# Normalising the first batch's attention on GpSimd, with the spread of the sums issued one row of maxima earlier

## The reference: one transformer layer with ternary weights

```
q, k, v = x@wqT+bq, x@wkT+bk, x@wvT+bv      # 16 heads of 8
attn    = softmax(q·k / 4) · v                # per head, over 1024 keys
x       = layernorm(x + attn@woT + bo)
h       = silu(x@w1T*s1) * (x@w2T*s2)         # 512 wide
h       = gelu(h@h1T*s); h = gelu(h@h2T*s)
out     = layernorm(x + h@w3T*s3)
```

## Time and profile before

| | us |
|---|---|
| median of 3 runs | 441.21 |
| lowest, highest | 440.68, 442.07 |
| the profiled execution | 441.35 |
| its span in the trace | 439.6 |
| granted TensorE clock, mean | 0.998 of full |

### The profile page before, as it was taken

The page is one execution under the profiler, slowest core; times in us unless marked ns, Lnnn a source line. Parts: engine busy times, 40 slices in busy tenths (PEclk is TensorE's granted clock), DMA queues, the critical chain, the costliest instruction groups (busy, mean ns, idle before and its releaser), DMA issues.

```text
span 439.6 us, 9789 instructions
## 1 busy us (share of the span) xinstructions
PE 426.9 (97%) x3498; PEld 228.3 (52%) x3498; DVE 383.8 (87%) x704; ACT 363.6 (83%) x683; POOL 106.9 (24%) x198
## 2 busy tenths in 40 slices
PE   8999999999999999999999999999999899999995
PEld 3544545444444444444445454544333588877884
DVE  6799999999999999999999999999874576657636
ACT  4497989999998999998899998998799885678762
POOL 9730110101011010101101013958111363046103
PEclk9999999999999999999999999999999999999999
DMA  5667741111131111113011111121021000000101
GB/s 161 174 204 119 281 147 28 49 28 28 48 123 25 40 37 28 28 48 123 25 40 39 26 28 49 16 41 52 10 41 49 15 8 1 1 1 3 48 1 48
DMA packets 17117, 24.89 MB, mean 57 GB/s; under 512 B 5168, under 2 KB 9008, under 8 KB 16688
## 3 DMA queue, kind: packets, MB, share of 16 engines
q1 hardware_dynamic: 16464, 23.68, 19.8%
q10 hardware_dynamic: 608, 0.59, 0.5%
HBM read 15.08 MB, written 7.60 MB: 52 GB/s over the span
## 4 chain that ended last, share of the span: by engine, by line
PE 74%; DVE 12%; ACT 4%; SPq 3%; issue 2%; DMA 2%; POOL 1%; POOLq 0%; DVEq 0%; ACTq 0%
PE ps L1366 23%; PE ps L1288 18%; PE ps L1476 16%; DVE negmax L983 11%; PE ps L1350 9%; ACT arena L663 2%; DMA parts_q<-arena 2%; PE ps L1220 2%; PE ps L1231 1%; PE ps L1420 1%; PE ps L1316 1%; PE ps L1260 1%; SPq L462 1%; SPq L434 1%; ACT v_pad L716 1%
## 5 line engine op out<-in xcount | busy, mean ns | idle before, releaser
L983 DVE TENSOR_REDUCE negmax<-ps 128x1 f32<-128x512 f32 x458 | 274.5, 683 | 1.4 <-PE ps L1288 1.3
L663 ACT ACTIVATE arena<-ps 128x512 f32<-128x512 f32 x360 | 190.3, 605 | 21.3 <-PE ps L1350 14.7
L1350 PE MATMUL ps<-qx,kx 64*128 64x512 f32 x512 | 170.0, 450 | 0.9 <-DMA qx<-mT 0.6
L1288 PE MATMUL ps<-kx,qx 61*128 61x512 f32 x468 | 159.3, 440 | 0.8 <-DMA qx<-parts_q 0.5
L1288 PEld LDWEIGHTS ps<-kx,qx 61*128 61x128 f32 x468 | 75.1, 184 | 86.7 <-DVE negmax L983 76.6
L1366 PE MATMUL ps<-arena,v_pad 128*32 128x256 f32 (+3 forms) x1328 | 104.7, 407 | 2.4 <-ACT arena L663 2.4
L663 ACT ACTIVATE hf<-ps 128x512 f32<-128x512 f32 x152 | 83.3, 602 | 9.5 <-PE ps L1350 8.0
L1350 PEld LDWEIGHTS ps<-qx,kx 64*128 64x128 f32 x512 | 78.6, 184 | 18.2 <-ACT arena L663 11.5
L1476 PE MATMUL ps<-hid,w_high 128*128 128x512 f32 (+1 forms) x296 | 68.3, 387 | 0.8 <-issue 0.4
L1476 PEld LDWEIGHTS ps<-hid,w_high 128*128 128x128 f32 x296 | 54.2, 188 | 12.4 <-issue 0.8
L1366 PE MATMUL ps<-hf,v_pad 128*32 128x128 f32 (+1 forms) x600 | 47.5, 388 | 0.0
(11 more groups left out here) (109 smaller groups left out, 333.7 us busy)
## 6 DMA issues: line engine op xcount, KB each, us to landing
qx<-parts_q SPq DMA_DIRECT2D x60, 64.0 KB, 2.1
late_sb<-in_late SPq DMA_DIRECT2D x3, 1280.0 KB, 5.7
kx<-parts_k SPq DMA_DIRECT2D x56, 64.0 KB, 2.1
parts_q<-prt SPq DMA_DIRECT2D x3, 512.0 KB, 6.4
parts_q<-arena SPq DMA_DIRECT2D x3, 512.0 KB, 8.2
xT_sb<-in_xT SPq DMA_DIRECT2D x4, 256.0 KB, 4.0
xT_sb<-arena SPq DMA_DIRECT2D x28, 32.0 KB
prt<-den SPq DMA_DIRECT2D x7, 128.0 KB
```

The costliest lines, as they stand in the source:

```text
L663: nc.scalar.activation(probs(n // HG)[:, heads(n), :], ps[:, PLAN["score", n][0], :], ACT.Exp, scale=SCALE).then_inc(exp_done, 1)
L983: nc.vector.tensor_reduce(negmax[:, t // TURNS % 2, m % 2, h * QT + q:h * QT + q + 1], ps[:, MAX_BANK + m % 4, :], AX.X, ALU.max, negate=T ...
L1288: nc.tensor.matmul(ps[:, half_bank(m), :], qx[at, slot, qc, h, q * P:(q + 1) * P], kx[at, slot, h, part * C:(part + 1) * C], start=True, s ...
L1350: nc.tensor.matmul(ps[:, bank, :], kx[at, slot, h % PAIR, kt * P:(kt + 1) * P], qx[at, slot, qc, h % PAIR, :], start=True, stop=True)\
```

## The change

GpSimd gets a function `norm(c)` with the two waits (sums spread back, attention moved) and the multiplication, and runs it for chunk 0 ahead of step 12 and for chunk 1 ahead of step 13 of its own list. VectorE loses `norm(0)` and `norm(1)` and keeps those of the second batch. SyncE issues `spread(0)` ahead of `load_max(ITERS - 1, 2)`.

```diff
+NORM_STEPS = (12, 13)
...
             load_max(ITERS - 1, 1)
             gather(0)
             move(0)
+            spread(0)
             load_max(ITERS - 1, 2)
-            spread(0)
             load_max(ITERS - 1, 3)
...
+            def norm(c):
+
+                if c == 0:
+                    pool.wait_ge(den_back[0], 16 * NG)
+                    pool.wait_ge(moved[0], MOVED[0])
+                at = slice(c * C, (c + 1) * C)
+                nc.gpsimd.tensor_tensor(attn_c[:, at], attn_c[:, at], den[:, at], ALU.mult)\
+                  .then_inc(chunk_normed, 1)
+
             for k in range(STEPS):
+                if k in NORM_STEPS:
+                    norm(NORM_STEPS.index(k))
                 if k % KT == 3 and k // KT + 1 < PER:
                     split_max(ITERS - 1, k // KT + 1)
...
             def norm(c):

-                if c == 0:
-                    dve.wait_ge(den_back[0], 16 * NG)
-                    dve.wait_ge(moved[0], MOVED[0])
                 if c == QC:
...
             dve.wait_ge(max_split, U_ALL)
-            norm(0)
-            norm(1)
             dve.wait_ge(pv_done, HF_STEPS)
```

## The result

| | before | changed |
|---|---|---|
| median, us | 441.51 (6 runs) | 444.72 (6 runs) |
| lowest, highest | 440.68, 442.07 | 444.26, 446.34 |
| ratio, 95% interval | | 1.0080 (1.0059 to 1.0100) |
| profiled execution, us | 441.35 | 444.55 |
| its span, us | 439.6 | 442.8 |

A forecast was written before the change was run, and what follows sets the result against it. The prediction took the chain through VectorE's maxima, the split and a normalisation before out_proj as the bound; +2.56 for the split less 0.57 for the normalisation gave +1.99, so 441.21 + 2.0 = 443.2 us, range 441.8 to 444.4.

The forecast's parts named there:

- The spread's start: On SyncE, the write of the sums to DRAM starts at about 293.74 us, not 299.26.
- From write to first read: On SyncE, 2.18 us from the write of the sums to the first read-back, at 295.92.
- The read-back: Four DMAs of the sums: 7.59 us from first issue to last packet plus 0.41 wake-up, so GpSimd starts at 303.92.
- GpSimd's chain: On GpSimd behind the wait: two multiplications at 1.23 us, five slices at 1.92 and a 0.05 tail, before the split.
- The split: GpSimd's split of unit 15's maxima starts at 316.03 us instead of 313.47, 2.56 late.
- Out_proj: On TensorE, out_proj starts 0.16 us behind the turn, at 318.29 against 316.30: 1.99 late.
- I carry the whole +2.0 to the end: Behind out_proj, the delay of 2.0 us reaches the end whole, with nothing made up by ScalarE or TensorE.
- VectorE's two multiplications: Taking 2 x 0.69 us from VectorE has value zero, as its flags now start when the split is done.
- Idle time that suffices: Rival: sums back on GpSimd by 301.36, split at 313.47 as before, 0.57 us won, time 440.6; chance 0.07.
- The stall partly made up: Rival: TensorE's 0.76 us of later idle time shrinks the 2.0 to 1.25, time 442.5; chance 0.13.
- The maxima's packets among the sums': Rival: unit 14's loads run among the sums' reads, sums and split 1.2 us later, +3.2, 444.4; chance 0.08.
- Unit 14's maxima as the bound: Rival: they land behind the sums, so late that TensorE stops at the group of 305.70; 444 or above; chance 0.03.

The follow-up runs named there:

- spread_only: The kernel before with only the spread of the sums issued ahead of unit 14's maxima load, both normalisations left on VectorE: 441.71 us against 441.65, ratio 1.0007.
- changed_again: The changed kernel run once more, unaltered, for a second profile: 444.05 us in one run.
- norms_late: The changed kernel with GpSimd's two normalisations ahead of its steps 18 and 19 instead of 12 and 13: 441.22 us against 441.65, ratio 0.9997.
- late_and_held: norms_late with SyncE waiting, before the load of unit 14's maxima, until the sums are back: 440.62 us in one run.
- loads_held: The changed kernel with SyncE waiting, before the load of unit 14's maxima, until the sums are back: 445.0 us in 4 runs, ratio 1.0089.
- pool_only: The changed kernel with the spread back behind the load of unit 14's maxima, normalisations still on GpSimd: 450.56 us against 441.21, ratio 1.0207.

## Why the prediction was wrong, step by step

The direction and the mechanism were right: the idle time of 7.48 us did not suffice, and the split moved from VectorE's chain to GpSimd's. Of the 3.97 us by which the end is late, 2.0 were forecast, 0.5 are missing at out_proj (the read-back), and 1.45 come behind it (the clock). Step by step, behind zero (forecast values less 278.82):

- **The spread's start.** Forecast 14.92, measured 14.91. Right, as was the move's price of nothing (spread_only).
- **From write to first read.** Forecast 2.18, measured 2.04. Between the two prices in the earlier trace rows.
- **The read-back.** "7.59 us from first issue to last packet" and 0.41: forecast 8.00, measured 8.82. Here the sum was mis-sized by 0.8. I had this as a rival with a chance of 0.08 and a price of 1.2, and dismissed it since the loads "are issued last". The profiles average 8.0 without loads behind and 8.8 with them. The Trainium skill (DMA: Bandwidth & Descriptors, Queues, rings and completion order) says that each engine takes its descriptors in ring order. I read this as if a later load could not slow the reads, which the page does not say; the measurement decides, and reads with a load issued behind them took longer. That its packets ran among theirs is not shown.
- **GpSimd's chain.** Forecast 12.11 from the first multiplication to the split, measured 12.03 (303.82 to 315.85). Each multiplication took 1.28 and its spacing was 1.23, as taken from the earlier trace rows.
- **The split.** Forecast 2.56 late, measured 3.15.
- **Out_proj.** Forecast 0.16 behind the turn, measured 0.10; 1.99 late against 2.52.
- **"I carry the whole +2.0 to the end."** This is the step that failed. It was right only that nothing is made up. I had read the clock in the earlier trace rows as 1.00 and taken it for granted, while my own sum put a 2.5 us hole into TensorE's stream. The hole cost 1.45 more (2.52 at out_proj, 3.97 at the end), and nothing more when it was filled (2.80 and 2.77). No rival priced it. Where the clock did not fall (changed_again), 2.39 at out_proj became 2.34 at the end, so the carry of the hole's own length was right.
- **VectorE's two multiplications.** Value zero, right: its flags started at 317.92, right behind the split.
- **The rivals.** Idle time that suffices: norms_late brings it about, by moving the wait and not by faster transfers, and there 0.3 of the gain reaches the end, not 0.57. The stall partly made up: no. The maxima's packets among the sums': its time, 444.4, is nearest to the measured one, but by luck, since the reads cost 0.8 and not 1.2, and the rest is the clock. Unit 14's maxima as the bound: not in the changed kernel, but it shows in late_and_held, where their load starts 5.5 us later still.

## What to carry to other kernels

A wait given to an idle engine delays everything queued behind it there. Compare the arrival of what it waits for with the due time of the last instruction behind it less all the work between, not with the engine's idle share; and put the wait behind as much of the other work as there is.

When a change makes TensorE wait for some microseconds, price the hole twice: by its length, and by the matmuls behind it at half clock, 1.45 to 1.83 us here where the clock fell. Before spending a gain on the chain, look at which engine is next: here half of it was given back at the scores that wait for ScalarE.

## What the runs showed of the hardware that I had not expected

- TensorE's granted clock (1.2 instead of 2.4 GHz) fell to half behind a hole of 3.1 us, of 3.6 us and of 2.0 us, and after 4.8 us inside one of 7.5. It stayed full behind one hole of 3.0 us, and behind holes of 0.5 us. What was added between out_proj and the end was 1.45, 1.52, 1.47 and 1.83 us. The Trainium skill (TensorE: Matmul & The Clock Gate, What's actually happening) says that the lower clock is the default, that activity releases it, and that the point of this transition varies. The traces agree that the clock falls where TensorE has idled, and show that the fall varies too: holes of 3.0 and 3.1 us of the same kernel ended differently.
- The clock can fall up to a us after TensorE has started again (0.3 us in the changed kernel, 1.0 in loads_held), so the wait itself may look undisturbed; in pool_only it fell inside the wait.
- Two small loads (12 KB each) issued behind four reads of 128 KB went with reads of 8.8 us on average (nine profiles), against 8.0 without them (three).
- The part ahead varies by over 2 us from execution to execution (the last load ahead of the change: 277.50 to 280.04); behind it, what was not changed agrees to 0.01 us over different kernels (the split of unit 15 at 34.64 to 34.66).
